# An expert stage in 28 steps of mixed block height instead of 36 equal steps

## The chip, the cores and the metric

The kernel runs on one core of one Trainium2 chip. The metric is the device time in microseconds (us) of one execution; lower is better. Three runs of the kernel before stand beside one profiled execution.

## The reference, cut to what matters

1250 rows of 512 numbers pass through a graph layer with attention and a linear-attention layer, and then through a feed-forward layer, which is the part that matters here. For each row (`h`, after a layer norm) a router picks the best 2 of 64 experts, and each expert is a small two-layer network of its own:

```python
r = h @ Wr
logits = r @ codebook.T / TEMP
probs = jax.nn.softmax(logits, axis=-1)
vals, idx = jax.lax.top_k(probs, K)                                # K = 2
w = vals / jnp.sum(vals, axis=-1, keepdims=True)
eh = jax.nn.silu(jnp.einsum('td,edf->tef', h, W1) + b1)            # W1: 64 x 512 x 256
eo = jnp.einsum('tef,efd->ted', eh, W2) + b2                       # W2: 64 x 256 x 512
moe = jnp.einsum('te,ted->td', combine, eo)
shared = (jax.nn.silu(h @ Ws1 + bs1) @ Ws2 + bs2) * SHARED_SCALE   # 512 -> 1024 -> 512
hmoe = (moe + shared).reshape(B, S, D)
f = silu(_ln(hmoe) @ Wf1 + bf1) @ Wf2 + bf2
```

There are 2500 pairs of row and expert. Counted on the reference's inputs, the experts get between 7 and 88 rows each.

## The kernel before, in words

The expert stage comes late in the kernel. The rows that one expert serves are cut into blocks of `R` = 64 rows, and an expert with any rows takes at least one block. On these inputs that gives 69 blocks. One step handles a **pair** of blocks side by side: 128 rows, 64 for each of two experts. `PAIRS0` = 36 steps are written out, and a loop in registers would add more if the routing asked for it; for 69 blocks it adds none, so 72 blocks are handled and three of them are empty.

Ahead of the steps a **preamble** turns the routing into lists. VectorE marks the two experts of each row (L999 to L1004, `m_made`), TensorE counts rows by expert and ranks each row within its expert (`rank`, L1686 to L1694), VectorE turns the counts into numbers of blocks and their first positions (L1011 to L1034), into the expert of each block (`owner`, L1044, which releases SyncE's weight loads), and into a position for each row (L1036 to L1066, `slots_made`). A matmul makes the lists (L1714), and with `gat_made` GpSimd may issue the first gathers (L624). TensorE runs eight groups of the shared network (`whole_hidden`) between these.

A step `p` of the loop (L1776 to L1788 on TensorE) consists of:
- `hidden(p)`, L1752: 4 contraction chunks times 2 blocks; each block is a tile of 64 columns of the array with its own weights `W1`, 256 numbers wide. Every such f32 matmul is two instructions in the trace.
- `result(p - 1)`, L1770: 2 chunks times 2 blocks, 512 wide, with `W2`.
- `BESIDE[p]`: parts of the shared network that `parts_beside` (L151) spreads over the steps by an estimated cost: 24 halves of `hidden` (L1659), 8 row tiles in three thirds each (`shared_rows`, L1670 and L1673), and 2 halves of `fb` (L1733).
- `hidden_transposes(p)` (L1760) and `transposes(p + 2)` (L1742): the latter turns rows that a gather brought.

Beside it VectorE copies (`hidden_kept`, L1098; `rows_turned`, L1092), ScalarE applies the activation block by block (L1348) and copies the result out (`eo`, L1356). GpSimd's queue (L626 to L635) takes, for each `p`: wait for `transposes(p)`, gather rows for `p + 2` into one of two buffers `Zg` (L614), wait until `result(p - 1)` was copied, scatter it (L619). SyncE's queue (`group_weights`, L490) has four buffers each for `W1` and `W2`, so two pairs' worth. It loads the weights of pair `p` once `hidden(p - 2)` is done (`W1`, L485) and once `result(p - 2)` is done (`W2`, L488), in this order in one queue. Each block needs two loads of 512 KB.

Behind the loop come the last two row tiles of the shared network, the reading back of the scattered rows (`Yt`, L515), and the last network `f`.

## Time and profile before

| what | us |
|---|---|
| runs, median of 3 | 886.72 |
| runs, lowest and highest | 884.51, 890.42 |
| profiled execution, its own time | 881.54 |
| profiled execution, span | 879.5 |
| first `hidden` of the loop starts | 539.90 |
| last `result` of the loop starts | 812.40 |

The span runs from the first to the last instruction of the trace. All times inside the trace count from the span's start. The execution's own time has 2.0 us around the span. The profiled execution is 5.2 us under the median of the three runs.

### The profile page before, as it was taken

Reading aid. Unit: us, or ns where it says so; the run is one execution under the profiler, and the core shown is the slowest. Engines: PE = TensorE matmul, PEld = TensorE weight load, DVE = VectorE, ACT = ScalarE, POOL = GpSimd, SP = SyncE. Lnnn points to the kernel's source line nnn. Section 1 sums busy time; section 2 is a strip of 40 time slices with the busy share of each in tenths; the row PEclk is TensorE's granted clock in tenths of the full one; section 3 lists DMA queues with packets and bytes.
Section 4 is the critical chain, followed back from the end, with each engine's and each line's share of the span. In section 5 each row is a group of like instructions: output and inputs, shape, how many; then the busy total and the mean of one; then the engine's idle time right before and its main releaser. Section 6 shows DMA issues by size and latency. Waiting matters only on the chain.

```text
span 879.5 us, 11949 instructions
## 1 busy us (share of the span) xinstructions
PE 843.0 (96%) x3978; PEld 490.5 (56%) x3978; DVE 513.0 (58%) x1312; ACT 290.0 (33%) x561; POOL 153.4 (17%) x174
## 2 busy tenths in 40 slices
PE   4999999999999999999999999999999999999988
PEld 2565556745577544444456586466456545654454
DVE  7687777666776999999755584222222222222472
ACT  4631111200105666656434332223122222222283
POOL 5100002400100000000000211344322222222340
PEclk9999999999999999999999999999999999999999
DMA  9310000000328250510211534789898988986722
GB/s 285 158 50 0 1 1 1 1 0 1 122 113 194 65 117 7 111 49 1 86 45 47 181 121 150 276 314 332 297 329 318 318 314 298 328 307 214 195 63 94
DMA packets 41340, 129.81 MB, mean 148 GB/s; under 512 B 8393, under 2 KB 8835, under 8 KB 40639
## 3 DMA queue, kind: packets, MB, share of 16 engines
q1 hardware_dynamic: 32955, 110.76, 38.8%
q0 software_dynamic: 7872, 17.94, 5.5%
q8 instruction: 33, 0.54, 0.2%
q10 hardware_dynamic: 452, 0.34, 0.1%
q14 instruction: 28, 0.23, 0.1%
HBM read 118.48 MB, written 19.68 MB: 157 GB/s over the span
## 4 chain that ended last, share of the span: by engine, by line
PE 64%; DVE 14%; DMA 7%; issue 5%; DVEq 5%; ACT 2%; POOLq 1%; SPq 1%; POOL 1%; ACTq 0%
PE ps L1492 8%; DVE att L941 7%; PE ps L1752 7%; PE ps L1770 6%; PE ps L1659 6%; PE ps L1673 5%; PE ps L1536 4%; PE ps L1624 4%; PE ps L1544 4%; DMA Zg<-z_d,gat 4%; PE ps L1451 3%; PE ps L1615 2%; PE ps L1587 2%; PE ps L1742 2%; PE ps L1823 2%
## 5 line engine op out<-in xcount | busy, mean ns | idle before, releaser
L1092 DVE TENSOR_SCALAR hgT<-ps,cols 128x128 f32<-128x128 f32 x152 | 51.8, 404 | 151.1 <-PE ps L1742 137.5
L941 DVE TENSOR_TENSOR att<-es,C 125x832 f32<-125x832 f32 (+1 forms) x120 | 116.3, 1011 | 4.6 <-ACT es L1271 3.9
L1271 ACT ACTIVATE es<-ps 125x832 f32<-125x832 f32 (+1 forms) x120 | 95.4, 867 | 54.7 <-PE ps L1576 53.8
L1587 PE MATMUL ps<-att,V 125*64 125x416 f32 (+1 forms) x480 | 96.7, 525 | 5.5 <-DVE att L941 4.3
L1673 PE MATMUL ps<-Ws_s,hsT 128*125 128x512 f32 x160 | 75.0, 607 | 0.0
L1659 PE MATMUL ps<-hT,Ws_s 128*128 128x250 f32 x320 | 72.8, 379 | 0.4 <-issue 0.4
L1492 PE MATMUL ps<-mW,xnT 128*125 128x512 f32 x160 | 72.2, 594 | 0.0
L1752 PE MATMUL ps<-W,hgT 128*64 128x256 f32 x576 | 70.1, 385 | 0.7 <-DVE hgT L1092 0.4
L1659 PEld LDWEIGHTS ps<-hT,Ws_s 128*128 128x128 f32 x320 | 58.9, 189 | 19.4 <-issue 13.2
L1770 PE MATMUL ps<-W,ehT 128*64 128x512 f32 x288 | 68.0, 592 | 0.7 <-ACT ehT L1348 0.7
L619 POOL DMA_INDIRECT y_d<-eo,lst x35 | 35.6, 1018 | 176.6 <-ACT eo L1356 176.6
L764 DVE TENSOR_SCALAR ohB<-iotaW,key 125x200 bf16<-125x200 f16 x320 | 64.9, 267 | 0.0
L1587 PEld LDWEIGHTS ps<-att,V 125*64 125x64 f32 x480 | 29.1, 136 | 56.1 <-issue 32.3
L1356 ACT COPY eo<-ps 128x512 f32<-128x512 f32 x36 | 21.1, 585 | 114.1 <-PE ps L1770 114.1
L1576 PE MATMUL ps<-Qst,Kst 128*125 128x416 f32 (+1 forms) x240 | 56.9, 370 | 1.7 <-DVE C L902 0.7
L1348 ACT ACTIVATE ehT<-ps,b1T 128x64 f32<-128x64 f32 x144 | 33.4, 317 | 74.5 <-PE ps L1760 74.5
L1576 PEld LDWEIGHTS ps<-Qst,Kst 128*125 128x125 f32 x240 | 41.2, 185 | 28.7 <-ACT es L1271 17.8
L1673 PEld LDWEIGHTS ps<-Ws_s,hsT 128*125 128x125 f32 x160 | 28.0, 187 | 46.0 <-issue 46.0
L1752 PEld LDWEIGHTS ps<-W,hgT 128*64 128x64 f32 x576 | 38.4, 136 | 20.6 <-DVE hgT L1092 0.6
L577 POOL DMA_DIRECT2D z_d<-yz x10 | 5.5, 548 | 235.6 <-DVE yz L976 235.4
L768 DVE TENSOR_TENSOR Cx<-Cx,ps 128x200 f32 x80 | 28.6, 358 | 29.5 <-PE ps L1451 16.8
L1451 PEld LDWEIGHTS ps<-ohB,ohA 125*128 125x128 bf16 x320 | 30.6, 113 | 27.1 <-issue 23.9
(251 smaller groups left out, 1198.0 us busy)
## 6 DMA issues: line engine op xcount, KB each, us to landing
W<-in_W SPq DMA_DIRECT2D x144, 512.0 KB, 7.1
Kst<-qk_d SPq DMA_DIRECT2D x32, 156.2 KB, 5.6
Qst<-qk_d SPq DMA_DIRECT2D x32, 156.2 KB, 5.9
Yt<-y_d SPq DMA_DIRECT2D x10, 448.0 KB
Ws_s<-in_Ws SPq DMA_DIRECT2D x2, 2048.0 KB, 9.7
qk_d<-qk_hi POOLq DMA_DIRECT2D x4, 625.0 KB, 3.5
qk_d<-qk_lo POOLq DMA_DIRECT2D x4, 625.0 KB, 4.7
z_d<-yz POOLq DMA_DIRECT2D x10, 250.0 KB, 2.7
```

Source lines behind the costliest of these rows:

```text
L764: i = V_.tensor_scalar(ohB[:, s, j, :], iotaW[:, :], key[:, bass.ds(k + j, 1)], None, ALU.is_equal)
L941: V_.tensor_tensor(att[:, n % AB, :, 0:w], es[:, n % EB, :, 0:w], C[:, s, o:o + w].unsqueeze(1).to_broadcast([P, 2, w]), ALU.mult).then_in ...
L1092: i = V_.tensor_scalar(hgT[:, u, k, :], bank(u, 128, 128, k * 128), col("g1", k), col("b1ln", k), ALU.mult, ALU.add)
L1271: S_.activation(es[:, n % EB, :, 0:w], scores_of(n, w), ACT.Exp, scale=float(DK) ** -0.5).then_inc(s_exp, 1)
L1451: i = MM(bank(b, WN), ohA[:, s, :, j], ohB[:, s, j, :], start=j == 0, stop=j == EG - 1)
L1492: i = MM(bank(b, D, P), xnT[:, k, t * P:t * P + P], mW[:, 1 + w, k, :], start=k == 0, stop=k == KD - 1)
L1576: k = MM(scores_of(n, w)[:, j, :], Kst[:, h % 4, s * P:s * P + P], Qst[:, h % 4, o:o + w], start=True, stop=True)
L1587: k = MM(sums_of(i, 64 * j, 64, w), V[:, s, pair, j:j + 2, :], att[:, n % AB, j, 0:w], start=s == 0, stop=s == T - 1, skip_group_check=True)
L1659: j = MM(bank(b, 250, 128, 250 * half), Ws1_s[:, k, (2 * g + half) * 128:(2 * g + half + 1) * 128], hT[:, k, c * 250:c * 250 + 250], start ...
L1673: i = MM(bank(b, D, P), hsT[:, t // 2 % 2, k, (t % 2) * P:(t % 2) * P + P], Ws2_s[:, k, :], start=False, stop=k == DSH // 128 - 1)
L1752: i = MM(bank(2, DFF, 128, DFF * u)[R * j:R * j + R], hgT[:, u, k, R * j:R * j + R], W1[2 * u + j][:, k, :], start=k == 0, stop=k == KD - ...
L1770: i = MM(bank(4 + u, D)[R * j:R * j + R], ehT[:, u, m, R * j:R * j + R], W2[2 * u + j][:, m, :], start=m == 0, stop=m == 1, skip_group_che ...
```

## The change

The rows of an expert are divided differently. Let the remainder be the rows left after the expert's full blocks of 64 (1 to 64). Where the remainder is at most 32, the expert is small, and the first 28 small experts get a block of 32 rows for it. Seven **quad** steps come first, each with four such blocks, four tiles of 32 columns. Then 21 pair steps follow as before. On these inputs exactly 28 experts are small, and together they place 564 rows in the quads (68 to 92 a step). The other 1936 rows fill 41 blocks of 64, and the pairs have room for 42. So 28 steps handle 70 blocks.

- TensorE: a quad step runs `quad_hidden`, the first part of `BESIDE`, both transposes, the other parts, and then `quad_result` of the same step, not of the one before.
- SyncE: a quad uses all four weight buffers. The four `W1` of a quad wait for `hidden` of the quad before, the four `W2` for its `result`.
- ScalarE: eight activations of 32 columns in a quad step, in place of four of 64.
- GpSimd: for each `p` the gather for `p + 2` is followed by the scatter of `p - 2`, not of `p - 1`.
- Preamble: a further small matmul and the instructions on VectorE that mark small experts, number them, and move the positions of the rows concerned.
- `BESIDE` gives a quad step a share of 4 and a pair step 1.4. `NP` falls from 52 to 44, `NB_MAX` stays 104.

```diff
-PAIRS0 = 36
-NP = 52
-NB_MAX = 2 * NP
+QUADS = 7
+PAIRS0 = QUADS + 21
+NP = 44
...
     ("rank", ["dve"] * 2),
+    ("small", ["dve"]),
+    ("rank", ["dve"]),
     ("base", ["dve"]),
...
     cost = {"hidden": 4 * 250, "shared": 3 * 512, "fb": 530}
-    total, done, table = sum(cost[p[0]] for p in parts), 0, [[] for _ in range(PAIRS0)]
+    share = [4 if p < QUADS else 1.4 for p in range(PAIRS0)]
+    total, done, table, p = sum(cost[p[0]] for p in parts), 0, [[] for _ in range(PAIRS0)], 0
     for part in parts:
-        table[min(PAIRS0 - 1, done * PAIRS0 // total)].append(part)
+        while p < PAIRS0 - 1 and done >= total * sum(share[:p + 1]) / sum(share):
+            p += 1
+        table[p].append(part)
         done += cost[part[0]]
     return table
...
-            def group_weights(h):
-
-                e = owners(h + 1)
-                for u in range(2):
-                    at_least(sp, h_done, 2 * h + u + 1)
-                    first_weights(e[2 * u], 2 * u)
-                    first_weights(e[2 * u + 1], 2 * u + 1)
-                    at_least(sp, e_done, 2 * h + u + 1)
-                    second_weights(e[2 * u], 2 * u)
-                    second_weights(e[2 * u + 1], 2 * u + 1)
-
-            for h in range(-1, PAIRS0 // 2 - 1):
-                group_weights(h)
+            def quad_weights(q):
+
+                e = owners(4 * q)
+                at_least(sp, h_done, q)
+                for j in range(4):
+                    first_weights(e[j], j)
+                at_least(sp, e_done, q)
+                for j in range(4):
+                    second_weights(e[j], j)
+
+            def pair_weights(p, u, e):
+
+                d = max(p - 1, QUADS) if isinstance(p, int) else p - 1
+                at_least(sp, h_done, d)
+                first_weights(e[0], 2 * u)
+                first_weights(e[1], 2 * u + 1)
+                at_least(sp, e_done, d)
+                second_weights(e[0], 2 * u)
+                second_weights(e[1], 2 * u + 1)
+
+            for q in range(QUADS):
+                quad_weights(q)
+            for p in range(QUADS, PAIRS0, 2):
+                e = owners(2 * p + 2 * QUADS)
+                pair_weights(p, p % 2, e[0:2])
+                if p + 1 < PAIRS0:
+                    pair_weights(p + 1, (p + 1) % 2, e[2:4])
...
             for p in range(PAIRS0):
                 gp.wait_ge(tr_done, p + 1)
                 gather(p % 2, gat[:, p + 2:p + 3])
-                if p:
-                    gp.wait_ge(e_read, p)
-                    scatter((p - 1) % 2, lst[:, p - 1:p])
+                if p >= 2:
+                    gp.wait_ge(e_read, p - 1)
+                    scatter(p % 2, lst[:, p - 2:p - 1])
                 if 2 <= p < 2 + T:
                     t = p - 2
                     gp.wait_ge(xy_kept, T)
                     nc.gpsimd.tensor_tensor(XR[:, t, :], XR[:, t, :], row("bf2"), ALU.add).then_inc(bf2_added, 1)
+            gp.wait_ge(e_read, PAIRS0 - 1)
+            scatter(PAIRS0 % 2, lst[:, PAIRS0 - 2:PAIRS0 - 1])
...
             reads("rank", 0)
-            V_.tensor_scalar(blkI[:, :], bank(TURNS.bank("rank", 0), P, E), float(R - 1), None, ALU.add).then_inc(dve_read, 1)
...
-            V_.tensor_scalar(nblk[:, :], blkI[:, :], 1.0, None, ALU.max)
+            reads_n = bank(TURNS.bank("rank", 0), 1, E)
+            V_.tensor_copy(cnt[:, 3:4], reads_n)
+            V_.tensor_scalar(cnt[:, 0:1], reads_n, float(R - 1), None, ALU.add).then_inc(dve_read, 1)
+            v.drain()
...
+            V_.tensor_scalar(smallb[:, :], cnt[:, 1:2].to_broadcast([E, P]), float(R // 2 - 1), None, ALU.is_le)
+            v.drain().then_inc(small_made, 1)
...
+            reads("small", 0)
+            b = TURNS.bank("small", 0)
+            V_.scalar_tensor_tensor(few[:, 3:4], bank(b, 1, E, E), float(4 * QUADS), few[:, 0:1], ALU.is_le, ALU.mult)
...
+            V_.tensor_scalar(nblk[:, :], few[:, 3:4].to_broadcast([E, P]), -1.0, few[:, 1:2], ALU.mult, ALU.add)
+            V_.tensor_scalar(full[:, :], few[:, 3:4].to_broadcast([E, P]), -128.0, few[:, 2:3], ALU.mult, ALU.add)
             v.drain().then_inc(blocks_made, 1)
...
             v.drain().then_inc(passed_made, 1)
...
+            V_.tensor_tensor(tmpr[:, :, :], rankS[:, :, :], full_s[:, :].unsqueeze(1).to_broadcast([P, T, E]), ALU.is_ge)
             V_.tensor_tensor(rankS[:, :, :], rankS[:, :, :], base_s[:, 0:E].unsqueeze(1).to_broadcast([P, T, E]), ALU.add)
...
+            V_.tensor_tensor(tmpr[:, :, :], tmpr[:, :, :], moved[:, :].unsqueeze(1).to_broadcast([P, T, E]), ALU.mult)
...
+            V_.tensor_tensor(rankS[:, :, :], rankS[:, :, :], tmpr[:, :, :], ALU.add)
...
                 hidden_kept(p, p % 2)
-                for name, t, part in BESIDE[p]:
-                    if name == "shared" and part == 2:
-                        shared_sum(t)
-                    if name == "fb" and part == 1:
-                        fold_last()
+                k = 1 if p < QUADS else len(BESIDE[p])
+                parts_read(BESIDE[p][:k])
                 rows_turned(p + 2, p % 2)
+                parts_read(BESIDE[p][k:])
...
+            def quad_turned(q, u):
+                a.wait_ge(x_done, q + 1)
+                at_least(a, e_done, q - 1)
+                for m in range(2):
+                    for j in range(4):
+                        i = S_.activation(ehT[:, u, m, 32 * j:32 * j + 32], bank(3, 32, 128, DFF * u + 128 * m + 32 * j), ACT.Silu,
+                                          bias=b1T[:, m, 4 * q + j:4 * q + j + 1])
+                i.then_inc(x_read, 1)
...
+            for q in range(QUADS):
+                parts_read(BESIDE[q][:1])
+                quad_turned(q, q % 2)
+                parts_read(BESIDE[q][1:])
+                result(q, q // 2, q % 2)
+            for p in range(QUADS, PAIRS0):
+                if p > QUADS:
+                    result(p - 1, (p - 1) // 2, (p - 1) % 2)
+                parts_read(BESIDE[p])
                 hidden_turned(p, p % 2)
...
+            pe.wait_ge(small_made, 1)
+            b = turn("small", 0)
+            MM(bank(b, E, P), smallb[:, :], triS[:, 0:E], start=True, stop=True)
+            MM(bank(b, 1, E, E), triI[:, :], smallb[:, 0:1], start=True, stop=True).then_inc(filled, 1)
+            rank(1)
             pe.wait_ge(blocks_made, 1)
             b = turn("base", 0)
             MM(bank(b, E + 1, P), nblk[:, :], triS[:, :], start=True, stop=True)
-            MM(bank(b, 1, E, E + 1), triI[:, :], nblk[:, 0:1], start=True, stop=True).then_inc(filled, 1)
-            rank(1)
+            MM(bank(b, 1, E, E + 1), triI[:, :], nblk[:, 0:1], start=True, stop=True)
+            MM(bank(b, E, P, E + 2), full[:, :], ident[0:E, 0:E], start=True, stop=True).then_inc(filled, 1)
+            rank(2)
...
+            def quad_hidden(q, u):
+                pe.wait_ge(tr_read, q + 1)
+                at_least(pe, h_read, q - 1)
+                for j in range(4):
+                    pe.wait_ge(w1_in[j], 16 * q + 16)
+                for k in range(KD):
+                    for j in range(4):
+                        i = MM(bank(2, DFF, 128, DFF * u)[32 * j:32 * j + 32], hgT[:, u, k, 32 * j:32 * j + 32], W1[j][:, k, :],
+                               start=k == 0, stop=k == KD - 1, skip_group_check=True)
+                i.then_inc(h_done, 1)
+
+            def quad_result(q, u):
+                pe.wait_ge(x_read, q + 1)
+                at_least(pe, e_read, q - 1)
+                for j in range(4):
+                    pe.wait_ge(w2_in[j], 16 * q + 16)
+                for m in range(2):
+                    for j in range(4):
+                        i = MM(bank(4 + u, D)[32 * j:32 * j + 32], ehT[:, u, m, 32 * j:32 * j + 32], W2[j][:, m, :],
+                               start=m == 0, stop=m == 1, skip_group_check=True)
+                i.then_inc(e_done, 1)
+
+            def loads(p):
+
+                return 16 * (QUADS + 1 + (p - QUADS) // 2)
...
+            for q in range(QUADS):
+                quad_hidden(q, q % 2)
+                parts_run(BESIDE[q][:1])
+                hidden_transposes(q, q % 2)
+                transposes(q + 2, q // 2 + 1, q % 2)
+                parts_run(BESIDE[q][1:])
+                quad_result(q, q % 2)
+            for p in range(QUADS, PAIRS0):
+                hidden(p, loads(p), p % 2)
+                if p > QUADS:
+                    result(p - 1, loads(p - 1), (p - 1) % 2)
+                parts_run(BESIDE[p])
                 hidden_transposes(p, p % 2)
                 transposes(p + 2, p // 2 + 1, p % 2)
```

## Rows read from the trace of the kernel before

**Rows 1.** The page: TensorE's busy time, and DMA share in 40 slices of the span.
```profile
PE 843.0 (96%) x3978; PEld 490.5 (56%) x3978; DVE 513.0 (58%) x1312; ACT 290.0 (33%) x561; POOL 153.4 (17%) x174
DMA  9310000000328250510211534789898988986722
```
**Rows 2.** Windows: stretch, engines' busy us (instructions), TensorE's granted clock, DMA share, GB/s.
```profile
539.90:812.40 272.50, 268.96 (x1424) 152.26 (x1425) 71.89 (x196) 62.91 (x203) 85.35 (x84) 1.00 0.85 299
...
520.50:531.00 10.50, 10.50 (x65) 9.46 (x64) 9.71 (x15) 3.18 (x7) 0.00 (x0) 1.00 1.00 379
```
**Rows 3.** The chain that ended last, in the loop: start us, us, what.
```profile
671.91 3.57 PE ps L1659 x16
```
**Rows 4.** The same chain from 690 to 708 us, one step and the next's start.
```profile
690.75 1.88 PE ps L1752 x16
692.63 1.72 PE ps L1770 x8
694.35 1.88 PE ps L1659 x8
696.23 1.05 PE ps L1670 x2
697.28 1.91 PE ps L1673 x4
...
699.90 1.88 PE ps L1752 x16
701.78 1.72 PE ps L1770 x8
703.49 2.77 PE ps L1673 x6
```
**Rows 5.** The weight tiles' instructions: duration ns min/median/max; last line, their DMAs.
```profile
L1752 PEld LDWEIGHTS ps<-W,hgT x576: 132/137/137, 539.9 to 805.9; 128*64 128x64 f32 x192
...
DMA to landing us min/median/max: 5.0/7.1/8.5
```
**Rows 6.** DMA traffic of the loop, 539.9 to 812.4 us: all packets; GpSimd's queue.
```profile
DMA packets 25285, 81.50 MB, mean 299 GB/s; under 512 B 5414, under 2 KB 5414, under 8 KB 25264
...
q0 software_dynamic: 5680, 9.91, 9.6%
```
**Rows 7.** Who waited for whom in the loop: us in total, times, longest.
```profile
PE ps L1742 <- DMA Zg<-z_d,gat: 1.9, 5, 0.6
...
PE ps L1752 <- DMA W<-in_W: 0.3, 1, 0.3
```
**Rows 8.** Timeline of the loop's end, all engines: start us, us, engine, line, operation.
```profile
802.55 1.02 POOL L619 DMA_INDIRECT y_d<-eo,lst  x1 [4.93 <-ACT eo L1356]
...
803.87 1.03 POOL L614 DMA_INDIRECT Zg<-z_d,gat  x1 [0.30 <-issue]
...
804.15 0.93 ACT L1348 ACTIVATE ehT<-ps,b1T 128x64 f32<-128x64 f32 x4 [2.40 <-PE ps L1760]
...
812.40 1.94 PE L1770 MATMUL ps<-W,ehT 128*64 128x512 f32 x8 [0.73 <-ACT ehT L1348]
```
**Rows 9.** Timeline of TensorE in the preamble.
```profile
513.59 0.69 PE L1693 MATMUL ps<-Mb,ones 125*125 125x64 bf16 x9
...
528.57 1.53 PE L1714 MATMUL ps<-slots,rowhot 125*128 125x156 bf16 x20
...
538.71 0.75 PE L1742 MATMUL ps<-ident,Zg 128*128 128x128 f32 x4 [0.28 <-DMA Zg<-z_d,gat]
```
**Rows 10.** Timeline of VectorE in the preamble.
```profile
511.23 0.22 DVE L1015 TENSOR_SCALAR nblk<-blkI 64x125 bf16<-64x125 int32 x1
...
514.38 0.49 DVE L1019 COPY rankS<-ps 125x320 f32<-125x320 f32 x1 [1.28 <-PE ps L1693]
...
515.86 0.83 DVE L1037 TENSOR_TENSOR tmpr<-M,rankS 125x640 f32<-125x640 f32 x1
...
525.49 2.39 DVE L1065 TENSOR_TENSOR slots<-slots,idh 125x1040 bf16<-125x1040 bf16 x2
```

More of the change, by code:

```diff
@@ L325, in block_kernel @@
         iotaB = ph("iotaB", [E, NB_MAX], F32, 131.5)
-        blkI = ph("blkI", [E, P], I32, 132)
+        cnt = ph("cnt", [E, 4], I32, 38.5)
+        few = ph("few", [E, 6], F32, 38.53125)
+        smallb = ph("smallb", [E, P], BF16, 59)
+        small_s = ph("small_s", [P, E], F32, 59.25)
+        full_s = ph("full_s", [P, E], F32, 59.5)
+        moved = ph("moved", [P, E], F32, 59.75)
+        full = ph("full", [E, P], F32, 132)
         nblk = ph("nblk", [E, P], BF16, 132.5)
@@ L1031, in _ @@
             v.drain().then_inc(passed_made, 1)
-            ranks(1)
+            V_.tensor_tensor(moved[:, :], moved[:, :], base_s[:, 0:E], ALU.subtract)
+            ranks(2)
             v.drain()
+            V_.tensor_tensor(tmpr[:, :, :], rankS[:, :, :], full_s[:, :].unsqueeze(1).to_broadcast([P, T, E]), ALU.is_ge)
             V_.tensor_tensor(rankS[:, :, :], rankS[:, :, :], base_s[:, 0:E].unsqueeze(1).to_broadcast([P, T, E]), ALU.add)
+            v.drain()
+            reads("owner", 0)
@@ L1035, in _ @@
+            v.drain()
+            V_.tensor_single_scalar(last[:, :], last_i[:, :], 2, ALU.logical_shift_right)
+            v.drain().then_inc(owner_made, 1)
+            V_.tensor_tensor(rankS[:, :, :], rankS[:, :, :], tmpr[:, :, :], ALU.add)
             v.drain()
@@ L1115, in fold_last, with parts_read @@
                 v.drain().then_inc(f1_folded, 1)
+            def parts_read(parts):
+                for name, t, part in parts:
+                    if name == "shared" and part == 2:
+                        shared_sum(t)
+                    if name == "fb" and part == 1:
+                        fold_last()
             rows_turned(0, 0)
@@ L1356, in result, with parts_read @@
                 S_.copy(eo[:, u, :], bank(4 + u, D)).then_inc(e_read, 1)
-            for p in range(PAIRS0):
-                if p:
-                    result(p - 1, (p - 1) // 2, (p - 1) % 2)
-                for name, i, part in BESIDE[p]:
+            def parts_read(parts):
+                for name, i, part in parts:
                     if name == "hidden" and part == 1:
                         shared_hidden(i)
+            for q in range(QUADS):
[7 more added lines that the diff above has]
+                parts_read(BESIDE[p])
                 hidden_turned(p, p % 2)
@@ L1685, in _ @@
             for q in range(T):
-                i = MM(bank(b, P, E), Mb[:, q, :], ones[:, 0:P], start=q == 0, stop=q == T - 1)
+                i = MM(bank(b, 1, E), Mb[:, q, :], ones[:, 0:1], start=q == 0, stop=q == T - 1)
             i.then_inc(filled, 1)
@@ L1689, in rank @@
                 b = turn("rank", 1 + c)
-                for t in range(5 * c, 5 * c + 5):
-                    o = (t - 5 * c) * E
+                for t in range(RANKS[c][0], sum(RANKS[c])):
+                    o = (t - RANKS[c][0]) * E
                     for q in range(t + 1):
@@ L1743, in transposes, with hidden @@
                 i.then_inc(tr_done, 1)
-            def hidden(p, g, u):
+            def quad_hidden(q, u):
[20 more added lines that the diff above has]
+                return 16 * (QUADS + 1 + (p - QUADS) // 2)
+            def hidden(p, n, u):
                 pe.wait_ge(tr_read, p + 1)
@@ L1761, in hidden_transposes, with result @@
                 i.then_inc(x_done, 1)
-            def result(p, g, u):
+            def result(p, n, u):
                 pe.wait_ge(x_read, p + 1)
@@ L1775, in _, with parts_run @@
             transposes(1, 0, 1)
-            for p in range(PAIRS0):
-                hidden(p, p // 2, p % 2)
-                if p:
-                    result(p - 1, (p - 1) // 2, (p - 1) % 2)
-                for name, i, part in BESIDE[p]:
+            def parts_run(parts):
+                for name, i, part in parts:
                     if name == "hidden":
```

84 lines of the change are left out of this document (51 added, 33 removed).

## The prediction, made before the changed kernel ran

> **What bounds the kernel now.** The page comes first: TensorE is busy 96% of the span, and in the last third, where the expert steps lie, the DMA engines are 80 to 90% busy too [rows 1]. So two resources must be priced. The windows separate the stage: from 539.90 to 812.40 us, 272.5 us, TensorE is busy for 268.96, at the full clock, and DMA at a share of 0.85 moves 299 GB/s [rows 2]. Busy matmuls overlap, so the third view is the chain of waits, whose pieces follow each other and can be added. In the loop it runs on TensorE from step to step: 1.88 us for `hidden`, 1.72 for `result`, then the parts, then 0.71 for both kinds of transposes (697.28 + 1.91 = 699.19 to 699.90) [rows 4]. A step's base is thus 4.31 us. A third of a shared row tile costs 2.77 us, the first one 1.05 + 1.91 = 2.96 [rows 4]. Two halves of shared hidden in a row cost 3.57 [rows 3], one by itself 1.88 [rows 4]. The eight row tiles cost 8 x 8.5 = 68.0, the 24 halves 12 x 3.57 = 42.8, and the two small `fb` parts I put at 2.0: 112.8 us.
>
> Check: 36 x 4.31 + 112.8 - 1.72 (the window ends where the last `result` starts) = 266.2 of 272.5 us. Of the missing 6.3, 3.5 is idle TensorE (272.5 - 268.96) [rows 2]: 0.73 before the last `result` [rows 8] and 2.8 mostly for gathers, seen at L1742, while the wait for weights is 0.3 us in all [rows 7]. The other 2.8 is loss at changes of the kind of matmul. TensorE bounds the loop, and DMA is covered by it, but not by much.
>
> **The pair steps that go.** 36 steps become 28. The parts stay the same, so TensorE loses 8 x 4.31 = 34.5 us, if a quad's matmuls cost what a pair's do.
>
> **A quad's matmuls.** `quad_hidden` has 32 instructions in place of 16, `quad_result` 16 in place of 8. In a pair, two 64-column tiles finish 16 instructions in 1.88 us, 118 ns each, while one full-width instruction of 250 columns takes 3.57 / 16 = 223 ns [rows 3, 4]: two tiles stream side by side. If four do, a quad costs 1.88 + 1.72, as a pair. That needs one weight load and matmul each 59 ns, and such pairs came 59 ns apart in the preamble ((0.69 - 0.22) / 8, where 0.22 us is one of them by itself) [rows 9], though in bf16. Loads of 64 columns take 137 ns and overlap [rows 5]. Lower bound: 3.6 us. Upper bound: nothing overlaps beyond what a full-width matmul does: 32 x 0.223 + 16 x 0.43 (1.72 / 4) = 14.0 us. I take 3.6, because the nearest row, two narrow tiles at the speed of one, shows no loss by the tiling. `quad_result` stands apart from `quad_hidden`, so each quad changes its kind of matmul once more, and a first block after a change costs at least 1.88 - 3.57 / 2 = 0.1 us more [rows 3, 4]; I take 0.2 x 7 = 1.4 us.
>
> The Trainium skill, in "TensorE: Matmul & The Clock Gate", section "Back-to-back issue gap", gives a sustained 81 ns per load-and-matmul pair at 128 columns, which speaks against four tiles at 59 ns. By it `quad_hidden` would take 32 x 0.081 = 2.6 us, 0.7 more, at most 5 us over seven quads; the 59 ns of the trace is under that figure, so I leave it out. "TensorEngine Tiling (Array Packing)", section "Key Properties", says that changing the tiling mode drains the engine; the trace agrees, with the 0.1 us just read.
>
> TensorE's work after: 28 x 4.31 + 112.8 - 1.72 + 1.4 = 233.2. Small losses scale, 2.8 x 28/36 = 2.2, and 0.73 remains before the last `result`: 236.1 us.
>
> **Weights, the resource that doesn't shrink.** 70 blocks in place of 72, 1.049 MB each. Eight loads (four blocks) come ahead of the loop as now. The loop's 81.50 MB [rows 6] become 66 x 1.049 + 9.9 (gathers and scatters, unchanged, [rows 6]) + 0.3 = 79.4 MB. While busy, the DMA engines moved 299 / 0.85 = 352 GB/s in the loop and 379 in the first burst of eight loads [rows 2]. So they need 210 to 226 us of a loop whose TensorE work is 236. They can't be covered well, since a quad holds all four buffers. Walk through it with: four `W1` have landed 8.5 us after being asked (the slowest landing, [rows 5]), or 5.9 us (2.1 MB at 352) behind the loads before them; four `W2` likewise, or 6.9 with the rows' traffic. The first quad's `hidden` ends at 0, its `result` at 0.71 + 8.5 + 1.9 = 11.1, after three thirds beside it. `W1` of quad 1 landed at 8.5, its `hidden` ends at 13.0, but its `W2`, asked at 11.1, land at 19.6. `W1` of quad 2 queue behind them until 25.5; TensorE was free at 24.1. Going on so, with 8.5, 7.1, 10.1, 5.5, 8.5 and 7.35 us of parts in quads 1 to 6, `hidden` ends at 27.4, 40.4, 55.0, 69.4, 82.4, and the last quad's `result` at 92.4. From the first `hidden`'s start that is 94.3 us against 87.1 of TensorE's work: 7.2 us of waiting, where it now has none. Of the first pairs, the second must have its `W1` loaded behind the first's: 2.3 us more. In the 21 pair steps the work is 4.31 + 57.2 / 21 = 7.0 us a step, and DMA needs 2.1 MB of weights and 0.37 MB of rows, 2.47 / 352 = 7.0 us. Two sets of buffers absorb jitter; I put 0.25 us of waiting on each step, 5 in all. Sum of the waits: 14.5; bounds 6 (379 GB/s) and 28 (330, and landings that spread more).
>
> Loop: 236.1 + 14.5 = 250.6 in place of 272.5: **-21.9 us**.
>
> **The later scatter.** Now the gather for `transposes(p + 2)` stands behind the scatter that waits for `eo`: it was issued at 803.87, after the scatter at 802.55 [rows 8], one step before it is wanted. Afterwards it goes out when `transposes(p)` ends, some 6 us earlier. So the 2.8 us of idleness at L1742 goes (already left out of the 236.1). The cost: the copy into `eo` waits for the scatter of two steps before, which is still issued one step after its result, so nothing. In a quad ScalarE has four activations more, 0.93 / 4 = 0.23 us each [rows 8], 0.93 in all, behind 5.5 us of parts. Where only 2.77 stand there (quad 4), they still fit.
>
> **The preamble.** VectorE is the chain from the marks to the lists. Added: three wide operations of 0.83 us (the kind of L1037), 0.9 each with a drain put at 0.07: 2.7; some 14 narrow ones and 5 drains more, of the kind of L1015, 0.22 us each, many of them overlapping: put at 2.0 [rows 10]. Gone: the 1.28 us in which VectorE waited for the second rank (filled by the new work), and 0.6 of `slots`, 44 wide in place of 52 (2.39 x 8/52 = 0.4 at L1065, the rest at L1059) [rows 10]. `slots_made` comes 2.8 later; TensorE's slack there is 0.6 us (VectorE done at 527.9, list matmul at 528.57) [rows 9, 10]. The gathers follow the lists, and the first transposes already wait for them [rows 9]. Cost 2.6 us; bounds 1 (most of it overlaps) and 5 (nineteen narrow operations at their full 0.22 = 4.2 in place of 2.0).
>
> **Behind the loop** nothing changes. **Sum**: -21.9 + 2.6 = -19.3. From the profiled execution's 881.5 that is 862.2. That execution stood 5.2 under the median, so in runs: 886.7 - 19.3 = **867.4 us**.
>
> **Rivals.**
> - *Tiles of 32 columns run only two at a time.* Speaks for it: no row has four. Each quad costs 3.6 us more, 25.2 in all, but it covers waits (to about 5): 236.1 + 25.2 + 5 = 266.3, a gain of 6.2, less 2.6: 883, within 1%.
> - *DMA governs the whole loop.* If bursts and gaps keep the mean at 299 GB/s [rows 2], 79.4 MB take 265.6 us from the first `hidden`'s end: a loop of about 269 and 886; at 320 GB/s 251 us, and 870. Against the worse end: the mean is 299 because TensorE sets the pace.
> - *Slower: the narrow tiles run one after another.* A quad's matmuls take 14.0 us, 10.4 over a pair's, 73 over seven quads: 236 + 73 + 0 = 309, and 886.7 + 36.5 + 2.6 = 926. It decides from the point where a quad's matmuls take twice a pair's 3.6 us: then gain and cost are about even. Against: the pair's speed.
> - *The split doesn't fit.* A routing with over 84 half positions would start the register loop, two more steps for 15 us: 882. On these inputs one block is spare, and a single expert crossing 32 rows is absorbed.
> - *Faster: hardly any waits.* At 379 GB/s waits of 4 to 6: 858.
>
> **How the numbers follow.** Chances: forecast 0.60, two at a time 0.10, DMA 0.11, one after another 0.04, not fitting 0.02, hardly any waits 0.13. A measurement of this kernel can tell about 1% (8.9 us) from no change. Faster by more: 0.60 + 0.13 + most of the DMA case = 0.82. Within 1%: two at a time, the rest of DMA, not fitting: 0.12. Slower: one after another and mishaps of its kind: 0.06. Range 857 to 880: the forecast with the bounds of waits and preamble, the fast case and half of the DMA case.
>
> **What would show it.** Right: quads in the chain at 1.9 and 1.7 us; the loop about 251 us long; TensorE waiting for weights (now 0.3 us) for 10 to 20 us, most in quads and the first pairs; DMA share above 0.9; L1742 without gather waits; the first `hidden` about 2.6 us later. Wrong: quad matmuls at 3.6 us or more, waits for weights over 30 us, or a first `hidden` 5 us later.

## Result, and the profile after

The changed kernel takes 865.32 us (median of 6 runs, 864.45 to 866.30), the kernel before 885.69 us (median of 6, 884.30 to 890.42): a ratio of 0.9765 with a 95% interval of 0.9743 to 0.9787. That is 20.4 us less; 19.3 were forecast. The profiled execution after has a span of 863.3 us against 879.5.

Three stretches tell where it came from. They are cut at the end of the marks on VectorE (`m_made`), the start of the first `hidden`, and the start of the last `result`. The windows of the changed kernel; the columns are those of [rows 2]:

```profile
511.26:545.60 34.34, 33.17 (x217) 29.02 (x217) 24.40 (x68) 9.09 (x20) 2.95 (x3) 0.90 0.37 133
545.60:793.52 247.92, 234.75 (x1352) 132.69 (x1353) 57.56 (x156) 55.55 (x191) 67.62 (x65) 0.99 0.87 319
793.52:863.30 69.78, 61.72 (x204) 35.86 (x204) 33.09 (x66) 31.01 (x53) 17.02 (x18) 0.95 0.42 115
```

The loop is 247.92 us long, where [rows 2] had 272.50. DMA moved 79.07 MB in it; 79.4 were forecast. The preamble takes 34.34 us, where the first profiled execution of before had 30.24 (509.66 to 539.90), and TensorE's granted clock is 0.90 in it; the part behind the loop takes 69.78 against 67.10. One profiled execution of each is not enough for the small stretches, as two more of the kernel before show below.

The weight tiles' instructions of the changed kernel, as in [rows 5] (L1847 and L1858 are the quads' `hidden` and `result`):

```profile
L1847 PEld LDWEIGHTS ps<-W,hgT x224: 106/110/178, 545.6 to 631.0; 128*32 128x32 f32 x112
L1847 PE MATMUL ps<-W,hgT x224: 376/379/634, 545.6 to 631.2; 128*32 128x256 f32 x112
L1858 PE MATMUL ps<-W,ehT x112: 589/592/617, 556.3 to 640.7; 128*32 128x512 f32 x112
...
  DMA W<-in_W: 12.3, 7
DMA to landing us min/median/max: 3.4/6.7/10.9
```

The wait for weights, 0.3 us before [rows 7], is now 12.3 us in 7 waits. The timeline of TensorE shows where (start, us, then what; in brackets the idle time just before and what ended it):

```profile
545.56 1.93 PE L1847 MATMUL ps<-W,hgT 128*32 128x256 f32 x32 [0.98 <-DVE hgT L1158]
...
556.25 1.92 PE L1858 MATMUL ps<-W,ehT 128*32 128x512 f32 x16
557.99 1.91 PE L1847 MATMUL ps<-W,hgT 128*32 128x256 f32 x32
...
568.66 1.92 PE L1858 MATMUL ps<-W,ehT 128*32 128x512 f32 x16
574.14 3.34 PE L1847 MATMUL ps<-W,hgT 128*32 128x256 f32 x32 [3.56 <-DMA W<-in_W]
...
602.13 1.93 PE L1847 MATMUL ps<-W,hgT 128*32 128x256 f32 x32 [0.70 <-DMA W<-in_W]
...
615.66 3.50 PE L1847 MATMUL ps<-W,hgT 128*32 128x256 f32 x32 [3.65 <-DMA W<-in_W]
...
642.15 1.95 PE L1874 MATMUL ps<-W,hgT 128*64 128x256 f32 x16 [0.90 <-DMA W<-in_W]
...
650.93 1.95 PE L1874 MATMUL ps<-W,hgT 128*64 128x256 f32 x16 [2.55 <-DMA W<-in_W]
```

Two things are to be read here. From start to start a quad's 32 instructions take 1.87 us (545.56 to 547.43) and its 16 take 1.74 (556.25 to 557.99), the time of a pair's 16 and 8, 1.88 and 1.72 in [rows 4]: four narrow tiles do run side by side. (The durations shown, 1.93 and 1.92, contain the modelled end of the last instruction.) And after the two waits of 3.6 us the same 32 instructions take 3.34 and 3.50 us: the granted clock is 0.57 from 574 to 578 us and 0.54 from 615.5 to 619.2, so it stood at its lower level, 1.2 GHz, for most of them.

### The profile page after: what moved, and what is told of

Same layout as the page of the kernel before. It is cut to its first block, busy times and chain, and to the rows that moved or that the text cites. A ratio compares the mean times of both kernels' runs of the same rounds, so it can differ in the third digit from the quotient of the medians.

```text
span 863.3 us, 11681 instructions
## 1 busy us (share of the span) xinstructions
PE 817.0 (95%) x3910; PEld 476.0 (55%) x3910; DVE 502.3 (58%) x1293; ACT 282.8 (33%) x549; POOL 137.0 (16%) x159
## 4 chain that ended last, share of the span: by engine, by line
PE 66%; DVE 11%; DMA 8%; issue 5%; DVEq 4%; SPq 2%; ACT 2%; ACTq 0%; POOL 0%; POOLq 0%
PE ps L1581 8%; DMA W<-in_W 7%; PE ps L1748 7%; DVE att L977 6%; PE ps L1762 5%; PE ps L1559 4%; PE ps L1625 4%; PE ps L1713 4%; PE ps L1874 4%; PE ps L1633 4%; PE ps L1892 4%; PE ps L1540 3%; PE ps L1676 3%; PE ps L1704 2%; PE ps L1955 2%
## 5 line engine op out<-in xcount | busy, mean ns | idle before, releaser
L1158 DVE TENSOR_SCALAR hgT<-ps,cols 128x128 f32<-128x128 f32 x120 | 40.9, 405 | 103.9 <-PE ps L1837 103.9
L1748 PE MATMUL ps<-hT,Ws_s 128*128 128x250 f32 x320 | 75.9, 393 | 0.4 <-issue 0.4
L1748 PEld LDWEIGHTS ps<-hT,Ws_s 128*128 128x128 f32 x320 | 62.1, 199 | 16.1 <-issue 8.8
L1676 PEld LDWEIGHTS ps<-att,V 125*64 125x64 f32 x480 | 29.1, 136 | 56.2 <-issue 32.1
L1164 DVE COPY eh<-ps 128x256 f32<-128x256 f32 x28 | 11.9, 425 | 63.8 <-PE ps L1847 41.5
L1437 ACT COPY eo<-ps 128x512 f32<-128x512 f32 x28 | 16.4, 586 | 96.4 <-PE ps L1892 67.3
L653 POOL DMA_INDIRECT y_d<-eo,lst x27 | 27.5, 1018 | 118.1 <-ACT eo L1437 118.1
L648 POOL DMA_INDIRECT Zg<-z_d,gat x30 | 31.0, 1032 | 94.1 <-PE ps L1837 60.9
L1874 PE MATMUL ps<-W,hgT 128*64 128x256 f32 x336 | 40.9, 385 | 4.5 <-DMA W<-in_W 4.3
L1581 PEld LDWEIGHTS ps<-mW,xnT 128*125 128x125 f32 x160 | 28.4, 188 | 29.0 <-issue 29.0
```

What stands on the lines that cost most here:

```text
L1158: i = V_.tensor_scalar(hgT[:, u, k, :], bank(u, 128, 128, k * 128), col("g1", k), col("b1ln", k), ALU.mult, ALU.add)
L1581: i = MM(bank(b, D, P), xnT[:, k, t * P:t * P + P], mW[:, 1 + w, k, :], start=k == 0, stop=k == KD - 1)
L1676: k = MM(sums_of(i, 64 * j, 64, w), V[:, s, pair, j:j + 2, :], att[:, n % AB, j, 0:w], start=s == 0, stop=s == T - 1, skip_group_check=True)
L1748: j = MM(bank(b, 250, 128, 250 * half), Ws1_s[:, k, (2 * g + half) * 128:(2 * g + half + 1) * 128], hT[:, k, c * 250:c * 250 + 250], start ...
L1874: i = MM(bank(2, DFF, 128, DFF * u)[R * j:R * j + R], hgT[:, u, k, R * j:R * j + R], W1[2 * u + j][:, k, :], start=k == 0, stop=k == KD - ...
```

## Experiments

Each kernel was timed in rounds with the kernel before, the last two excepted. "The changed kernel" is the one of the document's title.

### The scatter's order alone

```diff
 # on the kernel before
-                if p:
-                    gp.wait_ge(e_read, p)
-                    scatter((p - 1) % 2, lst[:, p - 1:p])
+                if p >= 2:
+                    gp.wait_ge(e_read, p - 1)
+                    scatter(p % 2, lst[:, p - 2:p - 1])
```

> The kernel before with the gather issued ahead of the later scatter, and nothing else changed. Theory (the 2.8 us of idle TensorE ahead of the transposes come from gathers that stand behind a scatter): these waits vanish from the trace and the time falls by 2 to 3 us, to about 883. Rival (the idle time moves to the next wait, or is noise): TensorE's idle time in the loop stays at 3 to 3.5 us and the time stays within 1 us of 885.7.

Measured: 881.44 us against 885.47, ratio 0.9959 (0.9938 to 0.9981), 3.6 us less by the ratio. Its loop, in the windows:

```profile
543.60:811.37 267.77, 266.67 (x1424) 152.16 (x1425) 71.86 (x196) 62.91 (x203) 85.18 (x84) 1.00 0.87 304
```

TensorE is idle for 267.77 - 266.67 = 1.1 us in place of 3.5, and no wait for a gather is left in the trace. The loop is 4.7 us shorter than in [rows 2], 3 to 4 shorter than in two further executions of before (below). So this small edit is about a fifth of the result. Its interval reaches from 1.7 to 5.5 us, so the runs alone can't tell 3.6 from the 2.8 us of idle time that were forecast. The trace can: TensorE's busy time falls too, from 268.96 to 266.67 us. A late gather shows only in part as idle time, as these two steps of the kernel before tell:

```profile
585.05 0.39 PE L1760 MATMUL ps<-ident,eh 128*128 128x128 f32 x2
585.27 0.65 PE L1742 MATMUL ps<-ident,Zg 128*128 128x128 f32 x4
...
591.24 0.39 PE L1760 MATMUL ps<-ident,eh 128*128 128x128 f32 x2
591.76 0.75 PE L1742 MATMUL ps<-ident,Zg 128*128 128x128 f32 x4
```

In the first the gathered rows are there, and the second kind of transposes starts 0.22 us behind the first. In the other it starts 0.52 us behind it, and no idle time is noted on PE, though the weight load of L1742 is marked as waiting for this gather. Nine of the 36 steps have such a distance, 0.38 to 1.00 us, together 4.0 us more than at 0.23. With the scatter moved the distance is 0.22 or 0.23 in all 36.

### The old order in the changed kernel

> The changed kernel with the gather behind the scatter of one step before, as in the kernel before. Theory (the order of the two is worth as much in the changed kernel as alone, where it gave 4.0 us): gather waits come back ahead of the transposes and the time is 868 to 870 against 865.3. Rival (the changed kernel waits for weights anyway, and these waits cover the gathers): 864 to 867.

Measured: 868.19 us, ratio 0.9837 (0.9792 to 0.9881); 2.9 us over the changed kernel and at the theory's 868 to 870. The two intervals only just miss each other (0.9792 against 0.9787). The loop is 250.96 us, 3.0 longer, and the waits that had gone are back (who waited for whom: us in total, times, longest):

```profile
PE ps L1835 <- DMA Zg<-z_d,gat: 2.9, 6, 1.0
```

Five of the six, 2.4 us, lie in the loop, all of them in pair steps. The two runs agree: the waits for weights, most of which fall in the quads and the first pairs, don't cover the gathers.

### The parts divided around the quad's result

```diff
 # on the changed kernel, TensorE; ScalarE's order likewise
-                parts_run(BESIDE[q][1:])
-                quad_result(q, q % 2)
+                parts_run(BESIDE[q][1:AHEAD[q]])
+                quad_result(q, q % 2)
+                parts_run(BESIDE[q][AHEAD[q]:])
```

`AHEAD` is 2, 2, 2, 3, 2, 2, 3: the first parts that make up half of a quad's cost, at least two.

> The changed kernel with about half of a quad's shared parts moved behind its result, so that the end of hidden and the end of result lie some 8 and 5 us apart in place of 11 and 2. Theory (the 12.2 us of waiting for weights come from the spacing of the two releases, in whose longer gap the DMA engines run dry): waits in the quads fall from 8.6 to under 3 us, the two quads that ran at a lower clock behind a wait of 3.6 us run at the full one, and the time is 855 to 858. Rival (the bytes alone set the quads' pace, 4.5 MB each at 352 GB/s or 12.8 us against 12.4 us of work): the waits stay within 2 us of what they are and the time is 864 to 866.

Measured: 853.91 us, ratio 0.9654 (0.9612 to 0.9696). That is 11.4 us under the changed kernel, with the same steps, bytes and instructions. Its loop and its largest waits for weights:

```profile
544.30:784.25 239.95, 234.75 (x1353) 131.09 (x1353) 57.62 (x156) 55.55 (x191) 67.71 (x65) 0.99 0.91 330
```
```profile
582.33 1.93 PE L1862 MATMUL ps<-W,hgT 128*32 128x256 f32 x32 [0.67 <-DMA W<-in_W]
...
607.25 1.93 PE L1862 MATMUL ps<-W,hgT 128*32 128x256 f32 x32 [0.54 <-DMA W<-in_W]
...
622.44 1.93 PE L1862 MATMUL ps<-W,hgT 128*32 128x256 f32 x32 [2.34 <-DMA W<-in_W]
...
626.92 3.32 PE L1763 MATMUL ps<-hT,Ws_s 128*128 128x250 f32 x8
```

Waits in the quads are 3.5 us (0.67 + 0.54 + 2.34) in place of 7.9 (the expectation's 8.6 is a little high), and waits for weights in the whole loop 4.1 in place of 12.3, which is the loop's gain. The DMA share rose from 0.87 to 0.91. So the number of bytes doesn't make these waits by itself, and the rival is out: most of them come of the bytes at this spacing of the two releases. The theory's point on the clock did not come true. TensorE is busy for the same 234.75 us, because the clock fell once more behind the wait of 2.34 us, which cost 1.6 us (the last line, 8 instructions that take 1.95 elsewhere, and a little of the next `result`), and because the rest of the busy time is 1.4 us more than in the changed kernel; the quads' parts now stand in more pieces. What the spacing looks like in the changed kernel is seen in its windows around the first quad's `result`, which starts at 556.25:

```profile
548.00:555.00 7.00, 7.00 (x22) 3.40 (x21) 1.37 (x4) 1.54 (x8) 1.01 (x1) 1.00 0.90 314
555.00:559.00 4.00, 4.00 (x40) 1.45 (x42) 0.69 (x1) 0.59 (x1) 0.00 (x0) 1.00 0.15 56
```

The next quad's `W1` has landed, and its `W2` may not be asked for until this `result` has ended: for 4 us the DMA share is 0.15, where it was 0.90 in the 7 us before.

The loop accounts for 8.0 of the 11.4 us. The other stretches of its profiled execution are 0.6 to 1.3 us shorter each, within what they vary by from one execution to the next (below), and the edit doesn't explain them. With the loop's part alone the time would be 857.3, inside the forecast 855 to 858; the 853.91 measured is 1.1 us under it.

### Half of the quads' weights

> The changed kernel where quads 1 to 6 load only half of each expert's weights (256 of 512 KB a load); it leaves out the other half. Theory (weights are what quads wait for, and the waits also cost clock): no waits for weights in the quads, no lower clock in them, 865.3 less 8.6 for waits and 3 for the clock, or 853 to 855. Rival (TensorE would then wait for something else, activations or row transposes): 860 or more, with new waits at quad_result or hidden_transposes.

```diff
 # on the changed kernel, quads 1 to 6; W2 likewise
-                    first_weights(e[j], j)
+                    (half_first if q else first_weights)(e[j], j)   # W1[s][:, 0:2, :] of W1[s][:, :, :]
```

Measured: 854.01 us, ratio 0.9651 (0.9613 to 0.9690). The quads have no wait for weights and run from the first to the last at 1.91 to 1.93 us. But the wait has partly moved on, to the second pair, whose full load starts behind the last quad's `result`:

```profile
627.89 1.95 PE L1880 MATMUL ps<-W,hgT 128*64 128x256 f32 x16
...
637.42 3.52 PE L1880 MATMUL ps<-W,hgT 128*64 128x256 f32 x16 [3.30 <-DMA W<-in_W]
```

So even with the quads' bytes halved the kernel is no faster than the divided one, which loads all of them. TensorE waits for no other engine in the quads, apart from 0.7 us ahead of the very first `hidden`. The time is inside the theory's 853 to 855.

### An earlier load at the change from quads to pairs

```diff
 # on the changed kernel, SyncE: order of the loads of pairs 7 and 8
+            e = owners(4 * QUADS)
+            at_least(sp, h_done, QUADS)
+            for j in range(2):
+                first_weights(e[j], 2 * (QUADS % 2) + j)
+            for j in range(2):
+                first_weights(e[2 + j], 2 * (1 - QUADS % 2) + j)
+            at_least(sp, e_done, QUADS)
...
-            for p in range(QUADS, PAIRS0, 2):
+            for p in range(QUADS + 2, PAIRS0, 2):
```

> The changed kernel with one change in SyncE's queue: the W1 loads of pair 8 are issued right behind those of pair 7, ahead of the W2 loads of pair 7, which wait for the last quad's result. Theory (the first pairs wait for weights because W1 of pair 8 stands behind that wait although its buffers are free): the 2.6 us of waiting at the second pair's hidden goes, 862 to 863.5. Rival (DMA has no room there, so the bytes come no earlier): 865.

Measured: 862.02 us, ratio 0.9737 (0.9704 to 0.9769). The second pair's wait of 2.55 us is gone and waits for weights are 9.6 us in all. The median is 3.3 us lower, but its interval overlaps that of the changed kernel, and the profiled execution has a loop as long as before the edit:

```profile
543.80:791.69 247.89, 237.47 (x1353) 132.48 (x1353) 57.58 (x156) 55.55 (x191) 67.70 (x65) 0.97 0.87 319
```

TensorE is busy for 2.7 us more at a clock of 0.97, which takes back what the wait gave. This stands behind the longest wait in the quads, which the edit doesn't touch:

```profile
614.28 3.64 PE L1858 MATMUL ps<-W,hgT 128*32 128x256 f32 x32 [3.64 <-DMA W<-in_W]
617.85 2.07 PE L1770 MATMUL ps<-b_s,combT 64*125 64x512 f32 x2
619.85 3.75 PE L1773 MATMUL ps<-Ws_s,hsT 128*125 128x512 f32 x4
```

The three groups take 1.93, 1.12 and 1.98 us at the full clock, so this one wait cost 4.4 us on top of its length; behind the like wait of 3.65 us in the changed kernel it was 1.6. The profiled execution is the slowest of the four runs. The time lies at the theory's 862 to 863.5, and the waiting is gone as it says; what that is worth in time is not settled.

> Both edits, the parts divided around the quad's result and the earlier W1 of pair 8. Theory: in the divided kernel the largest wait left is 2.3 us ahead of the last quad, not at the pairs, so the second edit adds under 1 us to the first: 853 to 854. Rival (the two add up, 853.9 less 2.5): 851 to 852.

Measured, both edits together: 854.75 us, ratio 0.9669 (0.9638 to 0.9700), the same as with the divided parts alone. The rival is out: the edits don't add up, as the theory said, though the figure itself lies 0.7 us over its narrow range.

### The parts spread evenly

```diff
 # on the changed kernel
-    share = [4 if p < QUADS else 1.4 for p in range(PAIRS0)]
+    share = [1 for p in range(PAIRS0)]
```

> The changed kernel with the shared parts spread evenly by step (share 1 for all) in place of 4 to a quad and 1.4 to a pair. Theory (weights set the quads' pace at 12.8 us a quad, so parts taken out of the quads only lengthen the pairs): quads stay at 12.5 to 13.5 us a step with 4 us of waiting for weights in each, pairs go from 7.1 to 8.3 us, and the time is 885 to 890, so the whole gain is gone although there are 28 steps. Rival (the gain is TensorE's 8 fewer steps, wherever the parts lie): 864 to 870.

Measured: 876.76 us, ratio 0.9914 (0.9886 to 0.9942). 11.4 us of the 20.4 are lost, not all. The quads' part of its timeline:

```profile
554.32 1.93 PE L1847 MATMUL ps<-W,hgT 128*32 128x256 f32 x32 [0.19 <-DMA W<-in_W]
...
563.89 3.64 PE L1858 MATMUL ps<-W,ehT 128*32 128x512 f32 x16 [4.16 <-DMA W<-in_W]
568.99 3.46 PE L1847 MATMUL ps<-W,hgT 128*32 128x256 f32 x32 [1.46 <-DMA W<-in_W]
...
581.72 1.93 PE L1847 MATMUL ps<-W,hgT 128*32 128x256 f32 x32 [1.16 <-DMA W<-in_W]
...
589.89 3.26 PE L1858 MATMUL ps<-W,ehT 128*32 128x512 f32 x16 [2.75 <-DMA W<-in_W]
595.62 3.29 PE L1847 MATMUL ps<-W,hgT 128*32 128x256 f32 x32 [2.48 <-DMA W<-in_W]
...
608.00 1.93 PE L1847 MATMUL ps<-W,hgT 128*32 128x256 f32 x32 [2.66 <-DMA W<-in_W]
...
620.58 3.27 PE L1847 MATMUL ps<-W,hgT 128*32 128x256 f32 x32 [2.82 <-DMA W<-in_W]
...
630.30 1.95 PE L1874 MATMUL ps<-W,hgT 128*64 128x256 f32 x16 [0.30 <-DMA W<-in_W]
```

From the first `hidden` at 544.10 to the first pair at 630.30 the seven quads take 86.2 us, 12.3 each, with only 29.1 us of parts between their matmuls. In the changed kernel they take 96.6 us (545.56 to 642.15), 13.8 each, with 53.9 us of parts. So 24.8 us less of work made the quads only 10.4 us shorter, and the pairs, which took the work over, went from 7.2 to 8.3 us a step as the theory said. The loop is 259.84 us long, 11.9 more: waits for weights are 19.0 us in place of 12.3, and TensorE is busy for 5.2 us more, mostly because the clock fell behind five of the waits (the five groups above over 3 us cost 7.3 us together, the changed kernel's two 3.0).

How far DMA is the floor here differs from quad to quad. The two between 595.62 and 620.58 take 12.4 and 12.6 us, with a DMA share of 0.97 and 0.99 in these windows:

```profile
600.00:612.00 12.00, 9.34 (x79) 6.38 (x78) 1.79 (x5) 2.95 (x11) 3.35 (x3) 1.00 0.97 368
612.00:624.00 12.00, 9.18 (x70) 5.41 (x69) 1.45 (x5) 2.95 (x11) 3.35 (x3) 0.86 0.99 382
```

From 552 to 600 us it is 0.88 to 0.95, so there the order of the releases still takes its part. The time the theory gave was too high by its own step lengths: 7 x 12.5 to 13.5 and 21 x 8.3 make a loop of 262 to 269 us, and 879 to 886, not 885 to 890. Neither theory is right as put: fewer steps and the scatter's order bring 9 us even so, and the other 11 hang on parts that stand where the loads are long.

### The preamble

```diff
 # on the kernel before, ahead of blocks_made, and behind the base is added to rankS
+            for i in range(5):
+                for j in range(3):
+                    V_.tensor_tensor(spare2[:, j:j + 1], ltri[0:E, j:j + 1], ltri[0:E, j:j + 1], ALU.add)
+                v.drain()
...
+            for _ in range(3):
+                V_.tensor_tensor(tmpr[:, :, :], M1[:, :, :], rankS[:, :, :], ALU.mult)
+                v.drain()
```

> The kernel before with 3 more wide and 15 more narrow VectorE operations and 5 more drains in the preamble, whose results are not used. Theory (VectorE is the chain of the preamble and 0.6 us of slack is all that covers it): the first hidden of the loop comes 3 to 4.5 us later against the end of the marks and the time rises by as much, to 889 to 890. Rival (TensorE's shared parts bound the preamble): under 1 us, 885 to 887.

Measured: 890.50 us, ratio 1.0055 (1.0024 to 1.0086), 4.9 us more, a little over the upper end that was expected. Two further executions of the kernel before tell how the stretch scatters by itself:

> The kernel before, unchanged, profiled once more. Theory (the profiled execution of before was a favourable one, since its clock was full in the preamble, while the kernel with only the scatter moved had 0.95 there and 2.7 us more): the preamble takes about 33 us at a clock of about 0.95, so the change itself costs 1 to 1.5 us there and not 4.1. Rival (the lower clock comes with the edits): 30.2 us at 1.00 again.

> As the run before it, to see how the preamble of one and the same kernel scatters. Both theories expect the same here as there.

The windows of the preamble, first the kernel with the added operations, then the two executions of before:

```profile
512.06:548.70 36.64, 33.73 (x211) 29.31 (x209) 24.51 (x66) 9.09 (x20) 2.87 (x3) 0.91 0.34 125
```
```profile
511.26:543.10 31.84, 30.76 (x208) 27.50 (x208) 20.69 (x47) 8.51 (x19) 2.95 (x3) 0.95 0.40 144
```
```profile
511.16:543.70 32.54, 31.54 (x211) 27.86 (x209) 20.66 (x47) 9.10 (x20) 2.92 (x3) 0.95 0.38 141
```

The kernel before takes 30.2, 31.8 and 32.5 us, and 32.9 with the scatter moved; a mean of 31.9, 31.5 without the last. The changed preamble takes 34.3 us, and 33.7 to 35.1 in the six kernels built on it, a mean of 34.2. So the change costs about 2.3 to 2.7 us here, between what the theory of the two further executions said (1 to 1.5) and the 4.1 that its rival would have kept. The added operations cost 4.7 to 5. VectorE's wait for the second rank grew to 2.4 us with them, from 1.3 in the kernel before; in the changed kernel it is gone.

What sets the length of this stretch is not what the prediction said. In the changed kernel VectorE has the lists ready at 532.58, but TensorE comes to the list matmul only at 534.42, behind 64 instructions of the shared network. The same 64 in the kernel before are the last line:

```profile
530.52 2.06 DVE L1131 TENSOR_TENSOR slots<-slots,idh 125x880 bf16<-125x880 bf16 x2
518.44 16.15 PE L1748 MATMUL ps<-hT,Ws_s 128*128 128x250 f32 x64
534.42 1.34 PE L1809 MATMUL ps<-slots,rowhot 125*128 125x132 bf16 x20
514.97 13.76 PE L1659 MATMUL ps<-hT,Ws_s 128*128 128x250 f32 x64
```

Neither group has a pause in it or behind it. The granted clock was 0.50 from 517.3 to 523.3 us in the changed kernel and 1.00 throughout in the first profile of the kernel before. In the changed kernel and the six built on it TensorE is the later one by 1.0 to 2.0 us. From the end of the marks these 64 start at 7.5 us (mean of the seven) in place of 5.8 (mean of the four profiles above of 30.2 to 32.9 us); from there to the start of the list matmul it is 15.5 us in place of 14.7, and what comes behind is 0.2 shorter: 1.7 + 0.8 - 0.2 = 2.3. The mean clock is 0.90 in all seven and 0.91 with the added operations, against 1.00 and three times 0.95. Whether the change brings this lower clock or the executions happened to fall so is not tested.

The loops of the two executions are 271.34 and 270.90 us:

```profile
543.10:814.44 271.34, 268.51 (x1425) 152.20 (x1425) 71.85 (x196) 62.91 (x203) 85.31 (x84) 1.00 0.85 300
```
```profile
543.70:814.60 270.90, 268.51 (x1424) 152.24 (x1425) 71.91 (x196) 63.08 (x203) 85.53 (x84) 1.00 0.86 301
```

So the mean loop of the three executions of before is 271.6 us, and the changed kernel's one is 23.7 us shorter.

## Why the prediction was right

**The sum.** Forecast -21.9 in the loop and +2.6 in the preamble, -19.3. Measured against the means of before: -23.7 in the loop, +2.3 to 2.7 in the preamble, and the part behind the loop between 67.1 and 69.9 us in before and after alike. Together about -21, and -20.4 in the runs. The mechanism, fewer steps against longer loads, came true. That the sum is within 1.1 us is partly luck, as the terms show.

**A quad's matmuls** cost what a pair's do, 1.93 and 1.92 us. The lower bound that was taken was right; 32 instructions in 1.9 us are 59 ns each, the spacing read from the bf16 matmuls of [rows 9]. One full-width instruction of 250 columns took 223 [rows 3]. The Trainium skill's "TensorEngine Tiling (Array Packing)", section "Theoretical Speedup", allows up to four times for 32 columns; the trace agrees, 223 against 59 ns is 3.8 times.

**TensorE's work** was put at 236.1 us with 0.73 of idle time, 235.4. Busy time was 234.75, of which 3.0 are the lower clock behind two waits (3.34 and 3.50 against 1.93). That leaves 231.8, the forecast's steps and parts (28 x 4.31 + 112.8 - 1.72) with nothing for its two small terms, 2.2 of loss at changes of the kind of matmul and 1.4 for the quads. The 2.2 was misread. It was scaled from the 2.8 us by which the loop of before exceeded pieces and idle time, and most of that belonged to the late gathers: busy time fell by 2.3 us, 1.8 against the two further executions of before, when only the scatter's order was changed. In the kernel with both edits, at a clock of 1.00, busy time is 233.2; there each quad's parts stand in more pieces. So about 1.4 us of loss of this kind can appear, but not in the kernel that was forecast.

**The waits for weights** were put at 14.5 us, measured 12.3, and their places were right only in part. The walk through the quads gave 7.2 us, 1.4, 1.4 and 4.4 ahead of quads 2, 3 and 5 (counted from 0); measured 3.56 + 0.70 + 3.65 = 7.9, ahead of quads 2, 4 and 5. It had the `hidden` of quads 1 to 6 end at 13.0, 27.4, 40.4, 55.0, 69.4, 82.4 us behind the first, and they ended at 12.4, 30.0, 41.5, 56.6, 71.7, 84.1 (559.83, 577.42, 588.89, 603.99, 619.09 and 631.49 less 547.43). The first pairs' 2.3 became 0.90 + 2.55 = 3.4. The 5 us that the pair steps were to wait came to 0.9. In the pairs TensorE is busy for 138.72 of 140 us and DMA still has a share of only 0.91:

```profile
653.00:793.00 140.00, 138.72 (x744) 78.28 (x740) 37.40 (x101) 34.50 (x112) 41.70 (x40) 1.00 0.91 330
```

While busy, DMA moved 330 / 0.91 = 363 GB/s there, not the 352 read from before, so 2.47 MB need about 6.8 us (an estimate) and not 7.0 of a step.

**What was missing.** The lower clock behind a long wait, 1.4 and 1.6 us here (3.34 and 3.50 against 1.93), was in no term. That it came to 3.0 us, and the two small terms that were not there to 3.6, is luck.

**The scatter's order** was put at 2.8 us; alone it gave 3.6, and 2.9 was lost by taking it back. In the trace it is worth 4.7 of the loop against [rows 2], 2.4 of idle and 2.3 of busy time; the forecast had only the idle part.

**The preamble** was put at 2.6 us, with VectorE as the chain and 0.6 us of slack on TensorE. VectorE's share was well sized: its lists are ready 3.0 us later by the means, 2.8 were forecast. But 2.8 less the slack is 2.2, so the 2.6 is 0.4 over its own terms, and TensorE, slower at the lower clock, set the time. The size is right by another way than the one forecast.

**The signs.** The loop (251 forecast, 247.9), the waits for weights (10 to 20, 12.3), the quads' matmuls and the transposes without gather waits are as the right case had them. A DMA share above 0.9 didn't come; it is 0.87, as the quads leave gaps. And one sign of being wrong did appear as written: the first `hidden` starts 5.7 us later than in the first profile of before (545.60 against 539.90). Of that 1.6 lie ahead of the marks, and two further executions of before start it at 543.10 and 543.70, so it says little; the sign should have been tied to the marks and to more than one execution.

**The rivals.** Two at a time and one after another are ruled out by the quads' 1.93 us. A second pass through the register loop didn't happen: L1874 has 336 instructions, 21 pairs of 16. The rival in which DMA governs the whole loop couldn't be told from the forecast by time: at 320 GB/s it had a loop of 251 us, which by its own terms is 867.8 and not the 870 written, and the mean measured is 319. The waits tell them apart: TensorE is idle for only 13.2 us, and in the pairs for 1.3 of 140. It is wrong for the pairs, and the evenly spread kernel shows single quads in which it decides. The rival of hardly any waits, 858, is out for this kernel with 12.3 us of them; the divided one, with 4.1, is at 853.9.

## What to carry to other kernels

When two blocks of half height share a step, count bytes as well as instructions: the matmul time per block was halved here, the bytes per block were not, so other work has to be moved to where the loads are long. Where one load waits for the first half of a step and another for the second, put the two releases half a step apart: at the same bytes and instructions this took 8 us out of the loop and 11 off the runs, about half as much as the whole change. And issue a transfer that the critical engine waits for ahead of one that it doesn't wait for in this stage: the gather ahead of the scatter gave 3 to 4 us for nothing. Where busy time exceeds the sum of its pieces, compare the starts of the pieces step by step before calling it a fixed loss: here it was a wait that the idle time didn't show.

## What the runs showed of the hardware

- Four tiles of 32 columns with weights and moving data of their own stream at once in f32: 32 instructions of 256 columns in 1.93 us, 59 ns each, where a full-width one of 250 columns took 223. A load of 32 columns takes 110 ns, one of 64 took 137 [rows 5].
- TensorE's clock fell to its lower level behind the longer waits of these rows, but the length alone doesn't tell when: 3.56 and 3.65 were followed by 3.34 and 3.50 us for 1.93 us of work, 2.48 by 3.29, 2.82 by 3.27, 4.16 by 3.64 for 1.92, while 2.55 and 2.66 were followed by the full clock. In the kernel with divided parts a wait of only 2.34 us was followed by the lower clock, at the work behind the quad's `hidden` (3.32 us for 8 instructions that take 1.95); between the two stood the 32 instructions of `hidden` at the full clock and 16 matmuls of one column each. Such matmuls with no wait ahead were followed by the full clock in the changed kernel (5.31 us for 24). Such a wait cost 1.3 to 1.7 us more than its length in the group right behind it, and once, behind 3.64 us, 4.4 in all.
- A late gather delayed the second transposes by up to 0.77 us a step, of which the trace of TensorE notes only a part as idle time: 4.0 us of delay in nine steps, 2.5 us of idle time at L1742.
- The same stretch of the same kernel had a mean clock of 1.00 in one execution and 0.95 in two others, where it took 1.6 and 2.3 us longer. The lower clock can come with no long pause of TensorE: in the changed kernel it was busy for all of the 6.0 us at 0.50, and for 3.81 of the 4 us before, with small matmuls. A difference of that size between two single profiles says nothing of a change.
